# One step of a hand-written order moved: the second experts inside the tenth pass, the last routing and its sends spread

## The reference, cut to what matters

```python
xn = _layernorm(x)
s = _L0_attn_ref(xn, ...)          # two halves, 8 heads each, layer norms, a feed-forward
g = _silu(_L0_ffn_ref(xn, ...))    # 16 experts, each token goes to one
x = x + s * g
xn = _layernorm(x)
s = _L1_attn_ref(xn, Wq, Wk, Wv, Wo)     # causal, 16 heads of 8
g = _silu(_L1_ffn_ref(xn, ...))    # 8 experts, each token goes to its best two
x = x + s * g
```

```python
logits = xt @ gate_w.T + gate_b
top_v, top_i = jax.lax.top_k(logits, TOP_K)          # TOP_K = 2, 8 experts
act = h0 * jax.nn.silu(h1)                           # of each expert
out = (softmax(top_v)[:, :, None] * sel).sum(axis=1)
```

## Time and profile before

| | |
|---|---|
| three runs | 1180.65, 1188.52, 1189.01 us, median 1188.52 |
| profiled execution | 1175.42 us, of which its span 1173.5 |
| TensorE matmul busy | 1005.4 us, 86% |
| VectorE, ScalarE, GpSimd busy | 787.6, 646.6, 576.8 us |
| mean granted TensorE clock | 0.922 of 2.4 GHz |

### The profile page before, as it was taken

How to read it: one execution, slowest core, us unless ns; L and a number is a source line. 1 busy time by engine, 2 the same in 40 slices (tenths; PEclk the granted TensorE clock), 3 DMA queues, 4 the chain that set the end, 5 groups by cost and what they waited for, 6 DMA issues and landing times.

```text
span 1173.5 us, 22918 instructions
## 1 busy us (share of the span) xinstructions
PE 1005.4 (86%) x7466; PEld 543.6 (46%) x7466; DVE 787.6 (67%) x2434; ACT 646.6 (55%) x1252; POOL 576.8 (49%) x670
## 2 busy tenths in 40 slices
PE   4757889998989898887988877777999899899888
PEld 2522269633333333332423444445888654444434
DVE  5597833488788887878777755674444587788741
ACT  1204732476767677665757643454444477667665
POOL 5266600155546373728678887741000264545564
PEclk8657989999999999999989988887999999999988
DMA  5852457662414050412323142234888544354221
GB/s 146 203 157 65 127 161 210 212 155 47 100 36 111 9 125 15 100 37 56 99 60 99 39 117 58 47 95 134 247 245 248 145 114 120 82 125 108 69 59 46
DMA packets 121864, 129.81 MB, mean 111 GB/s; under 512 B 13920, under 2 KB 104864, under 8 KB 121536
## 3 DMA queue, kind: packets, MB, share of 16 engines
q1 hardware_dynamic: 115184, 115.37, 37.9%
q0 software_dynamic: 6144, 12.60, 4.2%
q10 hardware_dynamic: 432, 0.52, 0.2%
HBM read 82.54 MB, written 52.35 MB: 115 GB/s over the span
## 4 chain that ended last, share of the span: by engine, by line
PE 56%; DVE 15%; issue 8%; POOL 7%; DMA 6%; ACT 4%; another core or an unknown queue 1%; SPq 1%; POOLq 0%; DVEq 0%; ACTq 0%
PE ps_banks L588 7%; PE ps_banks L629 7%; PE ps_banks L1810 5%; PE ps_banks L634 5%; DVE a_neg_max L888 4%; PE ps_banks L595 4%; DVE a_masked L894 3%; PE ps_banks L674 3%; PE ps_banks L1548 3%; PE ps_banks L1823 2%; PE ps_banks L1562 2%; PE ps_banks L726 2%; POOL sent L1673 2%; PE ps_banks L732 2%; PE ps_banks L640 2%
## 5 line engine op out<-in xcount | busy, mean ns | idle before, releaser
L777 ACT ACTIVATE a_probs<-ps_banks 128x512 f32<-128x512 f32 x512 | 278.9, 600 | 125.2 <-PE ps_banks L588 119.8
L588 PE MATMUL ps_banks<-q_strip,k_strip 53*128 53x512 bf16 (+3 forms) x1024 | 280.3, 352 | 67.5 <-DVE a_neg_max L888 24.4
L888 DVE TENSOR_REDUCE a_neg_max<-ps_banks 128x1 f32<-128x512 f32 x448 | 283.4, 682 | 63.8 <-PE ps_banks L595 57.2
L595 PE MATMUL ps_banks<-k_strip,q_strip 51*128 51x512 bf16 (+3 forms) x1024 | 289.2, 364 | 23.9 <-DVE a_neg_max L885 15.9
L894 DVE CUSTOM_DVE_ANT_0 a_masked<-ps_banks,mask_wide 128x384 bf16<-128x384 f32 (+3 forms) x512 | 223.8, 487 | 83.5 <-PE ps_banks L595 72.8
L779 ACT ACTIVATE a_probs<-ps_banks 128x512 f32<-128x512 f32 x256 | 144.5, 603 | 86.9 <-PE ps_banks L546 76.7
L1078 POOL DMA_INDIRECT tokens<-made,at x96 | 93.2, 971 | 178.1 <-DMA made<-work 126.0
L588 PEld LDWEIGHTS ps_banks<-q_strip,k_strip 53*128 53x128 bf16 x1024 | 72.6, 95 | 162.4 <-issue 60.3
L629 PE MATMUL ps_banks<-a_probs,v_aug 128*32 128x512 f32 x1024 | 139.7, 618 | 0.3
L595 PEld LDWEIGHTS ps_banks<-k_strip,q_strip 51*128 51x128 bf16 x1024 | 72.6, 95 | 131.3 <-ACT a_probs L777 62.4
L545 PE MATMUL ps_banks<-mask_kq,ident_halves 64*128 64x256 bf16 (+1 forms) x320 | 80.2, 261 | 0.3 <-issue 0.3
(11 more groups left out here) (259 smaller groups left out, 1753.2 us busy)
## 6 DMA issues: line engine op xcount, KB each, us to landing
work<-in_pack SPq DMA_DIRECT2D x39, 450.0 KB, 3.4
q_rows<-a_q_parts SPq DMA_DIRECT2D x96, 128.0 KB
k_rows<-a_k_parts SPq DMA_DIRECT2D x96, 128.0 KB
q_strip<-q_rows SPq DMA_DIRECT2D x64, 192.0 KB
k_strip<-k_rows SPq DMA_DIRECT2D x64, 192.0 KB
work<-in_w SPq DMA_DIRECT2D x32, 256.0 KB, 3.1
sent<-in_zeros SPq DMA_DIRECT2D x14, 512.0 KB, 8.0
work<-sent SPq DMA_DIRECT2D x55, 128.0 KB, 3.2
```

Of the source, the lines that this page charges most:

```text
L588: mm = pe.matmul(sbank[:, at:at + hi - lo], k_now[rows(js, ROW_END), slot, kt * P:(kt + 1) * P], q_now[rows(js, ROW_END), slot, lo:hi], st ...
L595: mm = pe.matmul(mbank[:, at:at + hi - lo], q_next[rows(jm, ROW_SHIFT), slot, qt * P:(qt + 1) * P], k_next[rows(jm, ROW_SHIFT), slot, lo:h ...
L777: act.activation(probs[si // 4 % 2][:, si % 4, :], bank, ACT.Exp).then_inc(sems["probs"], 1)
L888: dve.tensor_reduce(neg_max[:, half, qt, hd:hd + 1], bank, AX.X, ALU.max, negate=True).then_inc(sems["max_out"], 1)
```

## The change

Its core is four table lines. Passes 8 and 9 get other places, and pass 10 gets the last sends and the experts as a step.

```diff
 NEXT1 = {
-    **MISC[0], 1: [], 2: [("ln3a", -2)], 3: [("ln3b", -2)], 9: [], 11: [], 6: [("x2T", -2)], 7: [("logits", -2)],
+    **MISC[0], 9: [("x2T", -2)], 11: [("logits", -2)],
 }
...
-    NB: merged(routed(2, (13, 14, 15, 16), 17, (20, 21, 22), 25, 26, 27), sends(16, *2 * (0,), *2 * (7,), *2 * (17,), *2 * (23,))),
-    ROUTE1: merged(routed(3, (8, 9, 10, 11), 13, (15, 16, 17), 18, 19, 21), sends(24, *2 * (4,), *2 * (10,)), sends(28, *4 * (18,))),
-    **{MIX1 + i: mixed(-2, 8, 0, 18, 22, 24, 26, 28) for i in range(4)},
+    NB: merged(routed(2, (13, 14, 15, 16), 17, (20, 21, 22), 25, 26, 27), sends(16, *2 * (0,), *2 * (17,))),
+    ROUTE1: merged(routed(3, (13, 14, 15, 16), 18, (20, 21, 22), 24, 25, 26), sends(20, *2 * (0,), *2 * (7,), *2 * (12,), *2 * (19,), *2 * (27,))),
+    MIX1: merged(sends(30, *2 * (2,)), {10: [("experts1", 0, 0)]}, mixed(-2, 11, 12, 20, 24, 26, 28, 30)),
+    **{MIX1 + i: mixed(-2, 8, 0, 18, 22, 24, 26, 28) for i in range(1, 4)},
...
-                    if b == MIX1:
-                        experts1["tiles_sync"](sp)
                     for step in steps:
...
+                        if name == "experts1":
+                            experts1["tiles_sync"](sp)
...
+                        if name == "experts1":
+
+                            wait(pe, sems["probs"], n.at("probs"))
+                            wait(pe, sems["max_out"], n.at("max_out"))
+                            claim()
+                            experts1["tiles_tensor"](pe)
```

More of the change, by code:

```diff
@@ L368, in adds @@
         "gates": {}, "rstd0": {}, "choose0": {}, "count0": {}, "scan0": {}, "slots0": {}, "weigh0": {}, "send0": {}, "wide": {}, "fold": both,
-        "positions": {}, "masks": {}, "rest": {}, "choose": {}, "count": both, "place": {}, "weigh": {}, "send": {},
+        "positions": {}, "masks": {}, "rest": {}, "experts1": {}, "choose": {}, "count": both, "place": {}, "weigh": {}, "send": {},
     }
@@ L563, in _ @@
                         setup["masks_ready"](pe)
-                    if b == 1 or b == MIX1:
+                    if b == 1:
                         wait(pe, sems["probs"], n.at("probs"))
@@ L567, in _ @@
                         claim()
-                        (experts0 if b == 1 else experts1)["tiles_tensor"](pe)
+                        experts0["tiles_tensor"](pe)
                     for step in steps:
@@ L762, in _ @@
                         experts0["tiles_scalar"](act)
-                    if b == MIX1:
-                        experts1["tiles_scalar"](act)
                     for step in steps:
@@ L802, in _ @@
                             setup["gates_scalar"](act, arg)
+                        if name == "experts1":
+                            experts1["tiles_scalar"](act)
                         if name == "count0":
@@ L866, in _ @@
                         experts0["tiles_vector"](dve)
-                    if b == MIX1:
-                        experts1["tiles_vector"](dve)
                     for step in steps:
@@ L896, in _ @@
                                 op.then_inc(sems["max_out"], 1)
+                        if name == "experts1":
+                            experts1["tiles_vector"](dve)
                         if name == "choose0":
@@ L1022, in _ @@
                         experts0["done_pool"](pool)
-                    if b == MIX1:
-                        experts1["done_pool"](pool)
                     for step in steps:
@@ L1091, in _ @@
                                 pool.tensor_tensor(z[:], z_both[0][:], z_both[1][:], ALU.add).then_inc(sems["gate_in"], 1)
+                        if name == "experts1":
+                            experts1["done_pool"](pool)
                         if name == "rstd0":
```

## The result

The changed kernel takes 1198.74 us (median of 11 runs, 1191.77 to 1202.61), the kernel before 1185.91 us on the same chip (median of 11, 1179.03 to 1189.01). The ratio is 1.0106 with a 95% interval of 1.0079 to 1.0132: slower by 12.8 us (9.4 to 15.7). The forecast was 1192, at +4.3, with 1179 to 1204 as its range. The time is inside it; the sum fell short by 8.5 us. Every ratio in this document leaves out the executions of a kernel that lie over 1.5% above its fastest one, while the medians count all, so a ratio can differ a little from the quotient of the medians beside it.

What follows compares the result with a forecast made beforehand. The prediction took TensorE, busy 86% of the span, as the bound, through its standstills and clock. Gap +9.3, pass 9 -5, pass 8 and the rest 0 gave +4.3 us, forecast 1192 us, range 1179 to 1204.

Steps and rivals of the forecast that it cites:

- The gap: TensorE's idle stretch ahead of the experts: 14.5 us against 5.2 before, so +9.3 us, bounds +5.3 and +11.
- (a): First link from pass 10's k matmul start to the experts' first rows: the eviction of k, 1.8 us.
- (b): Second link ahead of the experts: GpSimd splits k into three parts, 3.9 us, sum 5.7.
- (c): Third link ahead of the experts: SyncE issues the six k copies, 3.75 us, sum 9.5.
- (d): Fourth link ahead of the experts: SyncE loads four register values and issues four packs, 3.85 us, sum 13.3.
- (e): Last link ahead of the experts: first rows issued and landed, 2.2 us, sum 15.5 if not queued behind packs.
- the queue's side: Ahead of the experts: rows land only after all packs on the same queue, at 18.4 us instead of 15.5.
- Pass 9: Waits for x2 and the count go, low clock goes, new waits come: -5 us, bounds 0 and -12.
- Pass 8: Sends of four tiles instead of eight, with no TensorE wait on GpSimd there: 0 us, bounds -3 and +1.
- The rest of pass 10: Mixing steps move behind the experts, TensorE waits for none of them: 0 us, bound +1.
- the slower rival: Gap pays the full chain, +11, pass 9 stays as it is, +2: +13, 1201 us; chance 0.19.
- The faster rival: Pass 9 falls to 45 us, pass 8 gives 3, gap +5.3: -9, about 1179; chance 0.07 beyond 12 us.

Runs made afterwards that it cites:

- e1: The changed kernel with the four weight packs issued at the head of pass 10, ahead of the copies; ratio 1.0026 to the kernel before, 1180.84 us.
- e4: The changed kernel with all places of passes 8 and 9 as before, only the experts' step and mixing as changed; ratio 1.0136, 1192.56 us.
- e3: The kernel before, experts at the head of pass 10, with the new tables of passes 8 and 9, last sends at place 31; ratio 1.0025, 1181.28 us.
- e6: e3 without the mixing steps of pass 10, so one output sequence is not written; ratio 0.9988 to the kernel before.
- e7: The kernel before with only sends changed: tiles 20 to 23 move from pass 8 to pass 9, 18 and 19 later in pass 8; ratio 1.0009.
- e8: e2 with the experts at place 5 of pass 10, last sends at place 0, mixing at its old places; ratio 0.9956 to the kernel before, 1179.21 us.
- e9: e8 with the experts at place 1 of pass 10 and the last four sends at place 31 of pass 9; ratio 0.9979 to the kernel before, 1177.71 us.
- e11: The kernel before run once more, unchanged, to see how far profiles differ; 1178.09 us.
- e5: e2 without the mixing steps of pass 10, so one output sequence is not written; ratio 0.9911 to the kernel before.
- e2: The changed kernel with packs and the first four row loads issued ahead of pass 10's q copies; ratio 0.9964 to the kernel before, 1173.72 us.
- e10: The same kernel as e2 run once more, unchanged, to see how far profiles differ; 1176.7 us.

## Why the prediction was right on the gap's mechanism and short by 8.5 us

- **The gap, mis-sized: +9.3 foreseen, +13.1 measured**, outside its bounds of +5.3 to +11. Every link was there, with k's start at 816.17 as zero. (a) The eviction ends at 1.8, as foreseen. (b) k's split ends at 6.2 instead of 5.7, since GpSimd was still at q's. (c) The k copies end at 10.2 (9.5): 0.5 us of that come from (b), and 0.2 since SyncE was still at q's. (d) SyncE spends 1.4 us between the last copy and the first pack; the row of 3.85 us that I had from the earlier trace rows begins with the first pack and leaves those loads out. The packs' issue itself takes 3.7 us, so (d) ends at 15.4 (13.3). (e) The rows take 5.9 us instead of 2.2: 21.4 in all, where the queue's side said 18.4. TensorE came 3.1 us after k's start, under the 3.4 to 5.0. e1 bears the sizes out: without the packs in the way 8.9 us of idle time go.
- **The choice between shared and ordered transfers.** I took 14.5 between 10.5 and 15.0. The rows did wait behind the packs, 5.9 us at a DMA share of 0.93 and 5.5 us in e4, against 2.2 to 2.5 us in the seven traces whose packs were issued long before (before, e3, e6, e7, e8, e9, e11). The ring order told of by the Trainium skill, page DMA: Bandwidth & Descriptors, section Queues, rings and completion order, agrees with that: the last pack landed at 837.0 and the rows were used at 837.55. The value at its end should have been taken.
- **Pass 9, -5 foreseen.** The two waits went, -6.8 (-6.0 foreseen), and the logits' wait came, 2.6 (2.9 foreseen). What I missed are two waits of 2.1 us for norms, at q and proj. Where the pass ends before an idle stretch, it is 55.0 and 55.3 us (e3, e6) against 56.5 and 57.5 (before, e11): -1.8, inside the bounds of 0 to -12. The clock stayed at 0.82; that the low clock would go with the waits, -6, was the step that failed. As many waits were left, in other places: 11.7 and 11.0 us in the pass 9 of before and e11, 11.1 and 12.1 in that of e3 and e6.
- **Pass 8, 0 foreseen, -3 to +1 as bounds.** Its sends did matter, -2.2 in the trace of the change, -3.6 in the mean over nine. I had looked for a wait on GpSimd in TensorE's waits and found none. That was the step that failed: the wait named after VectorE, 2.9 us for the logits, goes to 0.3 as soon as the sends beside it are gone (e7, where pass 8 has no other edit, and nine more traces). I had read it as the price of the pair logits and v. New waits took some of it back: in the means of nine and three traces TensorE's waits in pass 8 fall by 1.8 us in all (16.1 to 14.3) and its busy time by 1.7.
- **The rest of pass 10, 0 foreseen, +1 as bound: about +5.** This is the second large miss. The mixing, which I had costed, is not what costs most of it (e5). What does is only narrowed down. In the traces a cut one unit behind the boundary of the passes costs nothing (e9), one at place 5 or 10 does. In those kernels TensorE runs straight on from pass 9 into pass 10 and waits there for ScalarE and VectorE; an idle stretch at the boundary would let the two catch up for nothing (theory B). TensorE around that boundary, in the changed kernel and in e1:

```profile
803.33 0.39 PE L589 MATMUL ps_banks<-q_strip,k_strip 53*128 53x512 bf16 x1 [1.43 <-ACT a_probs_c L786]
...
808.60 0.33 PE L589 MATMUL ps_banks<-q_strip,k_strip 53*128 53x384 bf16 x1 [1.80 <-issue]
```

```profile
799.37 0.37 PE L592 MATMUL ps_banks<-q_strip,k_strip 53*128 53x512 bf16 x1 [1.07 <-DVE a_neg_max L902]
...
808.75 1.16 PE L684 MATMUL ps_banks<-a_z_T,wq 128*128 128x256 f32 x4 [2.95 <-DVE a_o_norm L933]
```

  These are 3 to 4 us of waits, some with a named releaser and one without, where before there was one idle stretch. That fits theory B, but isn't shown: more than half of the cost is longer busy time of TensorE, not wait, and e8's time is better than its trace. The cause of this term stays open.
- **The sum.** With the means above: idle +13.1, pass 8 -3.6, pass 9 -1.8, the cut +5.3: +13.0, against a measured +12.8. The same terms, each kernel with its own idle stretch, give +2.4, +4.0, -2.9 and -1.0 for e3, e1, e2 and e9, where the ratios say +2.9, +3.1, -4.2 and -2.5. They miss e8, +0.6 against -5.2. It was in part luck that the forecast was no further off: the gap (+3.8), pass 9 (+3.2) and the cut (+5.3) were all taken too low, and pass 8 (-3.6), taken at nothing, gave a part back.
- **The rivals and the signs.** What came is the slower rival (+13, 1201), which got 0.19. Both of its conditions were met: an idle stretch over 15 us (18.3) and a pass 9 not below 56 (58.3). It named the full chain and a pass 9 with no gain, and put its price of +2 on pass 9 instead of the cut. Of the signs, the packs behind the k copies, the end of the wait for x2 and the wait for the logits came; the idle stretch of 10 to 16 us and the pass 9 of about 51 us did not. One of the two signs of being wrong, a pass 9 above 57 us, came too. The chance for over 1% slower looks too small, since of three terms that the trace of before did not show, the loads and the cut were taken at nothing and the queue short of its upper end. The faster rival needed pass 9 at 45 us, and no kernel came near.

The experiments also point to a version that beats both: the change with packs and rows issued ahead (e2, 0.9964) or the experts at place 5 (e8, 0.9956). Both are 0.4% under the kernel before, with intervals that end just below 1.

## What to carry to other kernels

When a large step moves behind others, go through the queue of each engine that issues its loads: the step's first loads should be issued where they were, even if the computing moves. Of a chain of issues, count what lies between two groups of DMAs too (values loaded into registers), and give a small load behind large ones on the same queue the time of the large ones. When a trace names one engine for a wait, look at what the others did at that moment: here the wait for VectorE went when GpSimd's sends were moved. And a cut through a pass cost some 3 to 5 us here although no computation was added. A place where engines wait anyway may be one where others catch up for free, so compare several traces before giving such a term zero.

## What the runs showed of the hardware

- A load of rows (128 KB) was used 2.2 to 2.5 us after its issue where SyncE had issued nothing for 3 us or more (before, e3, e6, e7, e8, e9, e11), 2.9 us behind twelve copies of 128 KB (e1), 5.9 and 5.5 us behind those and four packs of 450 KB (the changed kernel, e4).
- The same instructions took 67.2 and 72.6 us in pass 8 of two executions of one program on two chips (e2, e10), at clocks of 0.89 and 0.84. The two spans differ by 3.9 us only (1170.9 and 1174.8).
- Thirteen more us of idle TensorE ahead of the experts did not slow the experts: 119.3 us at 0.97 as before.
- TensorE's wait for the logits in pass 8 was 2.9 us in three traces with four DMAs of GpSimd's sends beside it, and 0.3 us in ten without them.
